# Last layer of a fused four-layer kernel: the 32-point transforms as 32x32 array tiles, and the mode sums placed by VectorE and ScalarE

## The chip, the cores and the metric

The kernel runs on one core of one Trainium2 chip. The metric is the device time in microseconds (us) of one execution. Lower is better.

## The reference, cut to what matters

Four layers in a row, each `x = x + layer(groupnorm(x))` on x of shape (4, 32, 32, 32): a Volterra convolution, a 3x3 convolution, a gated attention layer, and the layer that the change touches, a two-dimensional discrete Hartley transform (DHT) convolution. M is the 32x32 matrix of the transform.

```python
def dht2(x, M1, M2):
    return jnp.einsum('bchw,kh,lw->bckl', x, M1, M2)

def neg_freq(a):
    return jnp.roll(jnp.flip(a, axis=(-2, -1)), shift=(1, 1), axis=(-2, -1))

def compl_mul2d(x1, x2):        # x1: transformed input, x2: weights1 (32, 32, 32, 32)
    x1n, x2n = neg_freq(x1), neg_freq(x2)
    return 0.5 * (einsum('bixy,ioxy->boxy', x1, x2) - einsum('bixy,ioxy->boxy', x1n, x2n)
                  + einsum('bixy,ioxy->boxy', x1, x2n) + einsum('bixy,ioxy->boxy', x1n, x2))
```

The product is transformed back with the same matrix. So for each of the 1024 modes (k, l) a 32-channel input is multiplied by a 32x32 matrix, once for the sum and once for the difference of a mode and its negative.

## The kernel before, in words

The program is written by hand: one instruction list for each engine (TensorE, VectorE, ScalarE, GpSimd, SyncE), tied together by semaphores. Nothing reorders it. Before the last layer come three others; the attention runs from about 90 to 280 us and ends with gates, cell and output of its last pieces. The `keep_clock(bank, n)` helper issues n matmuls of zeros, 128x512 in bf16 (L999), to keep TensorE busy where it would wait.

All of the state is on 128 partitions, image b and one of 32 indices on each group of 32. The last layer alternates a matmul that transforms the index on the partitions with a VectorE transpose of 32x32 blocks that brings the next index there:

- `t1` (L943): two transposes bring h to the partitions. They signal `t1_ready` 1 and 2.
- rows (L1261): for `mt` and `mrt` (the transform and its negative-frequency twin, block diagonal, 128x128), two matmuls of 512 columns each into banks 0 to 3. The i-th matrix signals `rows_done` i+1.
- `t2` (L949): two transposes of 128x1024.
- columns (L1270): for each matrix 16 matmuls with 32 output columns of the array and 256 moving columns, banks 4 to 7. They signal `cols_done` after every eight.
- `tu` (L958): eight transposes of 128x256 give U in `tmp3[:, 3]` and V in `tmp3[:, 4]`.
- mode parts (L458, `mode_part`): V+U and V-U are written into `xm`, a block diagonal tile of 8192 columns that GpSimd zeroed earlier. Each operation covers one 32-partition group g, 32x256 elements. `MODE_STAGES` are the four stages (k2, lh). VectorE makes six operations per stage and GpSimd two (`POOL_MODES = 2`).
- mode matmuls (L1285): in each of the four stages 32 matmuls of 64 columns on two array tiles of 64 columns, as soon as the stage's parts are there (`xm_dve`, `xm_pool`). Stages 0 and 1 end with `mix_done` 1, stages 2 and 3 with `mix_done` 2.
- `y1` (L970): four transposes of 128x1024, two after each `mix_done`. They signal `y1_ready` 1 to 4.
- inverse over l (L1301): five zero matmuls, then 32 matmuls of 256 columns, 16 for each s; each signals `inv_l_done`. The moving operand and the output are both read and written with gaps (last indices of the view: `k` outside `g` outside `s b`).
- `z1` (L976): a transpose of 128x1024 for each s.
- inverse over k (L1309): for each s two matmuls of 512 columns, accumulated; `inv_k_done` for each half.
- last transposes (L982) and the residual sum (L987), in two halves, each half stored by its own DMA.

Every f32 matmul stands in the trace as two records and two weight loads.

Of the kernel before, what the change touches and what calls it, by code (L numbers as in the profile page):

```python
# [45 lines left out]
P = 128  # L46
B, C, H, W = 4, 32, 32, 32
HW = H * W
# [75 lines left out]
POOL_MODES = 2  # L124
# [98 lines left out]
def build(nc, x, consts, wmodes, out):  # L223
    ctx = ExitStack()
    with ctx:  # L225
# [73 lines left out]
        z1 = arena_b[:, 4 * HW:6 * HW]  # L299

# [88 lines left out]
        xm_pool = sem("xm_pool")  # L389
# [58 lines left out]
        def mode_part(engine, k2, lh, g, part):  # L448

            rows = slice(32 * g, 32 * g + 32)

            half = slice(lh * MODES, (lh + 1) * MODES)
            dst = xm[rows].rearrange("p (jh k l) (jl m) -> p jh k (l jl) m", jh=2, k=2, jl=2)[
                :, :, k2, half, 8 * g + 4 * part:8 * g + 4 * part + 4]
            v = tmp3[rows, 4, :].rearrange("p (jh k n b) -> p jh k n b", jh=2, k=2, b=B)[:, :, k2, half]
            u = tmp3[rows, 3, :].rearrange("p (jh k n b) -> p jh k n b", jh=2, k=2, b=B)[:, :, k2, half]
            return engine.tensor_tensor(dst, v, u, ALU.subtract if part else ALU.add)  # L458
# [84 lines left out]
        def _(pool):  # L543
# [68 lines left out]
            pool.wait_ge(tu_ready, 8)  # L612
            pool.wait_ge(xm_zeroed, 1)
            for i, stage in enumerate(MODE_STAGES):
                for g in range(POOL_MODES):
                    if i or g:
                        pool.wait_ge(xm_pool, i * POOL_MODES + g)
                    mode_part(nc.gpsimd, *stage, g, 1).then_inc(xm_pool, 1)

        @block.scalar  # L620
        def _(act):
# [45 lines left out]
            for item in plan:  # L667
# [32 lines left out]
        def _(dve):  # L700
# [246 lines left out]
            for i in range(2):  # L947
                dve.wait_ge(rows_done, i + 1)
                nc.vector.transpose(tmp3[:, 1 + i, :].rearrange("p (c k) -> p c k", k=MODES),  # L949
                                    banks(2 * i).rearrange("p (w c) -> p c w", c=C)).then_inc(t2_ready, 1)  # L950

            for i in range(2):
                src = banks(4 + 2 * i).rearrange("p (b c k jl) -> p b k jl c", b=B, c=C, jl=2)
                dst = tmp3[:, 3 + i, :].rearrange("p (k l jl b) -> p b k jl l", b=B, l=MODES, jl=2)
                for b in range(B):
                    if b % 2 == 0:
                        dve.wait_ge(cols_done, 2 * i + b // 2 + 1)
                    nc.vector.transpose(dst[:, b], src[:, b]).then_inc(tu_ready, 1)  # L958
            dve.wait_ge(tu_ready, 8)
            dve.wait_ge(xm_zeroed, 1)  # L960
            for stage in MODE_STAGES:
                for g in range(4):
                    mode_part(nc.vector, *stage, g, 0).then_inc(xm_dve, 1)
                    if g >= POOL_MODES:
                        mode_part(nc.vector, *stage, g, 1).then_inc(xm_dve, 1)
# [8 lines left out]
            for s in range(2):  # L974
                dve.wait_ge(inv_l_done, s + 1)
                nc.vector.transpose(z1[:, s * HW:(s + 1) * HW].rearrange("p (o h l) -> p o h l", h=2, l=16),  # L976
                                    ps[:, 2 * s:2 * s + 2, :].rearrange("p h (o k) -> p o h k", o=C)
                                    ).then_inc(z1_ready, 1)

            for e in range(2):  # L980
                dve.wait_ge(inv_k_done, e + 1)
                link(nc.vector.transpose(  # L982
                    tmp3[:, 0, :].rearrange("p (k l) -> p l k", l=W)[:, e * W // 2:(e + 1) * W // 2],
                    ps[:, 4 + e, :].rearrange("p (o l) -> p l o", o=C)))
# [6 lines left out]
        def _(pe):  # L991
# [265 lines left out]
            keep_clock(7, 16)  # L1257
            for i, m in enumerate(("mt", "mrt")):
                for e in range(2):
                    pe.wait_ge(t1_ready, e + 1)  # L1260
                    last = mm(ps[:, 2 * i + e, :], c_(m), tmp3[:, 0, e * HALF:(e + 1) * HALF], start=True, stop=True)  # L1261
                last.then_inc(rows_done, 1)

            for i, m in enumerate(("mt", "mrt")):
                pe.wait_ge(t2_ready, i + 1)
                src = tmp3[:, 1 + i, :].rearrange("p (c k) -> p c k", k=MODES)
                for b in range(B):
                    for g in range(4):
                        dst = ps[32 * g:32 * g + 32, 4 + 2 * i + b // 2, (b % 2) * 256:(b % 2 + 1) * 256]
                        last = mm(dst.rearrange("p (c k) -> p c k", k=KG), c_(m)[:, 32 * b:32 * b + 32],  # L1270
                                  src[:, :, KG * g:KG * (g + 1)], start=True, stop=True)
                    if b % 2:
                        last.then_inc(cols_done, 1)

            keep_clock(3, 11)
# [14 lines left out]
            yv = y1.rearrange("p (k jl o g s b) -> p s b jl o g k", k=2, jl=2, o=C, g=4, s=2)  # L1291
            pe.wait_ge(y1_ready, 2)
            keep_clock(0, 5)
            for s, m in enumerate(("mt", "mnt")):
                for jl in range(2):
                    pe.wait_ge(y1_ready, 3 + jl)
                    for jh in range(2):
                        j = 2 * jh + jl
                        zv = ps[:, 2 * s + jh, :].rearrange("p (o g k j) -> p j o g k", g=4, j=2, k=2)
                        for b in range(B):  # L1300
                            last = mm(zv[32 * b:32 * b + 32, jl], c_(m)[:, 32 * j:32 * j + 32], yv[:, s, b, jl],  # L1301
                                      start=(jl == 0), stop=True, skip_group_check=True)
                last.then_inc(inv_l_done, 1)

            for s in range(2):
                pe.wait_ge(z1_ready, s + 1)
                zs = z1[:, s * HW:(s + 1) * HW].rearrange("p (o l) -> p o l", l=W)
                for e in range(2):
                    last = mm(ps[:, 4 + e, :].rearrange("p (o l) -> p o l", o=C), c_(("mt_back", "mnt_back")[s]),  # L1309
                              zs[:, :, e * W // 2:(e + 1) * W // 2], start=(s == 0), stop=(s == 1))  # L1310
                    if s == 1:
                        last.then_inc(inv_k_done, 1)

# [25 lines left out]
def layout_consts(i):  # L1339
# [46 lines left out]
    order = np.arange(MODES).reshape(4, 2, 4).transpose(1, 0, 2).reshape(-1)  # L1386
# [20 lines left out]
```

## Time and profile before

| | |
|---|---|
| median of 3 runs | 336.43 us (334.37 to 336.48) |
| the profiled execution's own time | 334.88 us |
| its span, first to last instruction | 333.1 us |
| mean granted TensorE clock | 0.95 |
| TensorE busy | 294.6 us (88%) |
| VectorE busy | 216.6 us (65%) |
| ScalarE busy | 175.2 us (53%) |
| GpSimd busy | 40.7 us (12%) |

### The profile page before, as it was taken

How to read it: one execution, taken by the hardware profiler on the slowest of the kernel's cores; microseconds unless marked ns; L12 is line 12 of the kernel's file. 1: busy time of each engine (PE TensorE's matmuls, PEld its weight loads, DVE VectorE, ACT ScalarE, POOL GpSimd, SP SyncE). 2: the span in 40 equal slices, each digit the busy share in tenths (PEclk: the TensorE clock that was granted, in tenths of full speed). 3: DMA queues.
4: the chain of work that ended last, by engine and by line, in shares of the span. 5: the costliest groups of instructions: out<-in, count | busy, mean ns of one | idle time of the engine just before them, and what ended most of it. 6: DMA issues, size and time to landing. Idle time of an engine off the chain costs nothing. (4 is left out here: it accounts for less than half of the span.)

```text
span 333.1 us, 9964 instructions
## 1 busy us (share of the span) xinstructions
PE 294.6 (88%) x4276; PEld 136.8 (41%) x4283; DVE 216.6 (65%) x484; ACT 175.2 (53%) x338; POOL 40.7 (12%) x50
## 2 busy tenths in 40 slices
PE   5799979899886499999999999999997998895993
PEld 2477523234313144444444454344342323344831
DVE  3991172478296236687979978888773223779935
ACT  1201101225194279798898989889797983100000
POOL 8400000000000000010101001010200108007000
PEclk9799999999996569999999999999999999997898
DMA  7100000005687559500000000000000000000001
GB/s 230 70 4 4 4 10 0 3 0 162 171 145 113 138 141 293 244 2 5 2 5 2 3 4 2 4 4 2 4 2 4 3 0 2 0 2 2 4 0 63
DMA packets 3471, 15.40 MB, mean 46 GB/s; under 512 B 731, under 2 KB 1547, under 8 KB 2883
## 3 DMA queue, kind: packets, MB, share of 16 engines
q1 hardware_dynamic: 3171, 14.67, 16.3%
q8 instruction: 33, 0.54, 0.7%
q0 software_dynamic: 256, 0.11, 0.2%
q14 instruction: 11, 0.09, 0.1%
HBM read 12.21 MB, written 2.37 MB: 44 GB/s over the span
## 5 line engine op out<-in xcount | busy, mean ns | idle before, releaser
L675 ACT ACTIVATE arena_b<-ps 128x512 f32<-128x512 f32 x232 | 124.9, 609 | 23.7 <-PE ps L1169 22.5
L1140 PE MATMUL ps<-arena_a 72*32 72x450 bf16 x1024 | 91.4, 376 | 4.7 <-DMA arena_a<-q_scratch 4.5
L1169 PE MATMUL ps<-arena_a 75*32 75x512 bf16 x896 | 88.9, 390 | 7.2 <-DMA arena_a<-mt_sb 6.3
L882 DVE TENSOR_REDUCE mx<-ps 128x1 f32<-128x450 f32 x120 | 68.6, 616 | 2.0 <-PE ps L1140 1.9
L877 DVE CUSTOM_DVE_ANT_0 sums<-ps,relus 128x450 bf16<-128x450 f32 x68 | 41.4, 626 | 35.2 <-PE ps L1140 26.8
L1187 PE MATMUL ps<-arena_b,vt 128*32 128x512 f32 x448 | 59.4, 602 | 1.5 <-ACT arena_b L675 1.0
L1140 PEld LDWEIGHTS ps<-arena_a 72*32 72x32 bf16 x1024 | 30.1, 101 | 42.2 <-issue 18.6
L1169 PEld LDWEIGHTS ps<-arena_a 75*32 75x32 bf16 x896 | 25.6, 97 | 52.4 <-ACT arena_b L675 20.6
L683 ACT ACTIVATE relus<-ps 128x450 f32<-128x450 f32 x68 | 37.5, 555 | 9.1 <-PE ps L1140 9.0
L1029 PE MATMUL ps<-arena_a,cst 32*32 32x512 f32 x864 | 30.0, 624 | 2.0 <-ACT arena_a L626 2.0
L999 PE MATMUL ps<-zeros 128*128 128x512 bf16 x82 | 21.3, 397 | 6.5 <-DMA xa<-x 3.5
L1029 PEld LDWEIGHTS ps<-arena_a,cst 32*32 32x32 f32 x864 | 21.4, 105 | 10.2 <-issue 4.9
L1187 PEld LDWEIGHTS ps<-arena_b,vt 128*32 128x32 f32 x448 | 13.8, 111 | 11.9 <-ACT arena_b L675 3.1
L596 POOL DMA_DIRECT2D arena_a<-mt_sb x8 | 5.2, 650 | 105.1 <-DVE mt_sb L891 105.1
L632 ACT ACTIVATE arena_b<-ps 128x512 f32<-128x512 f32 x4 | 2.2, 595 | 28.0 <-PE ps L1029 28.0
L743 DVE SCALAR_TENSOR_TENSOR arena_a<-xp 128x612 f32<-128x612 f32 (+1 forms) x24 | 16.2, 753 | 0.0
L1088 PE MATMUL ps<-arena_b,cst 128*32 128x450 f32 (+1 forms) x144 | 15.9, 565 | 0.0
L999 PEld LDWEIGHTS ps<-zeros 128*128 128x128 bf16 x89 | 8.0, 100 | 18.6 <-issue 7.7
L1285 PE MATMUL ps<-arena_b,arena_a 128*64 128x64 f32 x256 | 10.5, 258 | 4.0 <-DVE arena_a L458 4.0
L603 POOL TENSOR_TENSOR on<-ot,rden 128x512 f32<-128x512 f32 x7 | 7.3, 1039 | 51.6 <-DVE rden L901 51.6
L458 DVE TENSOR_TENSOR arena_a<-arena_a 32x256 f32<-32x256 f32 x24 | 12.9, 563 | 0.5
L899 DVE STREAM_TRANSPOSE ot<-ps 128x512 f32<-128x512 f32 x8 | 5.7, 712 | 10.1 <-PE ps L1193 10.1
(140 smaller groups left out, 237.2 us busy)
## 6 DMA issues: line engine op xcount, KB each, us to landing
arena_b<-wmodes SPq DMA_DIRECT2D x1, 4096.0 KB, 20.5
arena_a<-k_scratch SPq DMA_DIRECT2D x3, 516.8 KB
arena_a<-q_scratch SPq DMA_DIRECT2D x3, 384.0 KB
cst<-consts SPq DMA_DIRECT2D x1, 1045.0 KB, 9.3
k_scratch<-arena_b SPq DMA_DIRECT2D x3, 344.5 KB, 3.7
cst<-consts SPq DMA_DIRECT2D x1, 864.5 KB, 7.2
arena_a<-k_scratch SPq DMA_DIRECT2D x6, 129.2 KB
arena_a<-k_scratch SPq DMA_DIRECT2D x3, 258.4 KB
```

The costliest lines, as they stand in the source:

```text
L458: return engine.tensor_tensor(dst, v, u, ALU.subtract if part else ALU.add)
L675: nc.scalar.activation(probs[:, n % PRING, :], ps[:, SCORE_RING[n % len(SCORE_RING)], :], ACT.Exp).then_inc(expd, 1)
L683: nc.scalar.activation(relus[:, d % 3, :], ps[:, block_bank(i), 0:KHALF], ACT.Relu).then_inc(max_relu, 1)
L743: nc.vector.scalar_tensor_tensor(maps[:, m, n0:n1], xp[:, n0:n1], VOLTERRA_SCALE, xp[:, at + n0:at + n1], ALU.mult, ALU.mult).then_inc(map ...
L877: nc.vector.tensor_tensor_reduce(out=sums[:, d % 2, :], in0=bank, in1=relus[:, d % 3, :], scale=1.0, scalar=-3.0e38, op0=ALU.add, op1=ALU.max,
L882: nc.vector.tensor_reduce(mx[:, a, e:e + 1], bank, AX.X, ALU.max).then_inc(max_read, 1)
L999: mm(ps[:, bank, :], zeros[:, 0:P], zeros[:], start=True, stop=True)
L1029: last = mm(ps[32 * j:32 * j + 32, 2 * b + e, :].rearrange("p (y x) -> p y x", x=W), l0w[r, COL_TILES * i + j, :], window(maps[r, m, :], p ...
L1088: last = mm(ps[32 * b:32 * b + 32, bank + e, 0:ny * cols].rearrange("p (y x) -> p y x", x=cols), weights[:, px, :], window(xst[:, b, :], f ...
L1140: last = mm(ps[32 * j:32 * j + 32, block_bank(i), 0:KHALF], qst[0:PAIR_ROWS, e, g, q0:q0 + 32], kst[0:PAIR_ROWS, g, at:at + KHALF], start= ...
L1169: last = mm(ps[32 * j:32 * j + 32, bank, :], kst[0:S_ROWS, g, k0:k0 + 32], qst[0:S_ROWS, e, g, :], start=True, stop=True)
L1187: last = mm(ps[32 * h:32 * h + 32, bank, :], vt[:, t, half % B * HEADS + h, :], probs[:, (n0 + h) % PRING, :], start=(t == 0), stop=False, ...
```

## The change

Everything before the last layer is left as it was. In the last layer:

- rows: 64 matmuls on 32x32 array tiles, 128 columns each, replace four of 512. Row group b of the array writes bank 4i+b.
- columns: 32 matmuls on 32x32 tiles, 256 columns each, replace 32 that used all 128 rows. `cols_done` comes once for each matrix. The results lie in the upper halves of the eight banks. The zero matmuls behind them now wait for `tu_ready` 4.
- `t2`, `tu`, `z1` and the last transposes read across four banks with other strides. Their number and size are the same.
- mode parts: sum and difference are each made once per stage on 128 partitions (`both_parts`, 128x256 elements, into `xboth`). Then each 32-partition group's 512 elements are copied to their place in `xm` (`placed`): groups 0 and 1 by VectorE, 2 and 3 by ScalarE. GpSimd takes no part.
- inverse over l: 64 matmuls on 32x32 tiles, 128 columns each (`over_l`, 8 in a call). The first two calls need only `y1_ready` 2; ten zero matmuls of 256 columns follow them.
- inverse over k: 32 matmuls on 32x32 tiles, 256 columns each. Both last transposes wait for the same `inv_k_done`.

```diff
-        def mode_part(engine, k2, lh, g, part):
...
-            dst = xm[rows].rearrange("p (jh k l) (jl m) -> p jh k (l jl) m", jh=2, k=2, jl=2)[
-                :, :, k2, half, 8 * g + 4 * part:8 * g + 4 * part + 4]
...
+        def stage_of(tile, k2, lh):
+            return tile.rearrange("p (jh k n m) -> p jh k n m", jh=2, k=2, n=2 * MODES)[
+                :, :, k2, lh * MODES:(lh + 1) * MODES]
+        def both_parts(engine, k2, lh, part):
+            dst = stage_of(xboth, k2, lh)[:, :, :, B * part:B * part + B]
+            return engine.tensor_tensor(dst, stage_of(tmp3[:, 4, :], k2, lh), stage_of(tmp3[:, 3, :], k2, lh),
+                                        ALU.subtract if part else ALU.add)
+        def placed(k2, lh, g):
             rows = slice(32 * g, 32 * g + 32)
+            dst = stage_of(xm[rows].rearrange("p n m -> p (n m)"), k2, lh)[:, :, :, 2 * B * g:2 * B * (g + 1)]
+            return dst, stage_of(xboth[rows], k2, lh)
...
+            act.wait_ge(xm_zeroed, 1)
+            for i, stage in enumerate(MODE_STAGES):
+                act.wait_ge(both_ready, 2 * i + 2)
+                for g in ACT_PLACED:
+                    dst, src = placed(*stage, g)
+                    nc.scalar.activation(dst, src, ACT.Copy).then_inc(xm_act, 1)
...
             for i, m in enumerate(("mt", "mrt")):
                 for e in range(2):
                     pe.wait_ge(t1_ready, e + 1)
-                    last = mm(ps[:, 2 * i + e, :], c_(m), tmp3[:, 0, e * HALF:(e + 1) * HALF], start=True, stop=True)
+                    for q in range(4):
+                        for b in range(B):
+                            r, n = slice(32 * b, 32 * b + 32), slice(16 * 8 * e, 16 * 8 * (e + 1))
+                            last = mm(ps[32 * q:32 * q + 32, 4 * i + b, n].rearrange("p (w c) -> p w c", c=8),
+                                      c_(m)[r, r], t1[r, e * W // 2:(e + 1) * W // 2, 8 * q:8 * q + 8],
+                                      start=True, stop=True)
                 last.then_inc(rows_done, 1)
...
+            pe.wait_ge(tu_ready, 4)
             keep_clock(3, 11)
...
-                pe.wait_ge(xm_dve, (i + 1) * (8 - POOL_MODES))
-                pe.wait_ge(xm_pool, (i + 1) * POOL_MODES)
+                pe.wait_ge(xm_dve, (i + 1) * len(DVE_PLACED))
+                pe.wait_ge(xm_act, (i + 1) * len(ACT_PLACED))
...
+            def over_l(s, k, jl):
+                weights = c_(("mt", "mnt")[s])
+                for jh in range(2):
+                    j = 2 * jh + jl
+                    r = slice(32 * j, 32 * j + 32)
+                    for q in range(4):
+                        dst = ps[32 * q:32 * q + 32, 4 * s + j, 0:256].rearrange("p (b o g k) -> p k (o g) b", b=B, o=8, g=4)
+                        last = mm(dst[:, k], weights[r, r], yv[r, s, k, jl, 8 * q:8 * q + 8].rearrange("p o g b -> p (o g) b"),
+                                  start=True, stop=True)
+                return last
+            over_l(0, 0, 0)
+            over_l(0, 0, 1)
+            for _ in range(10):
+                mm(ps[:, 3, 256:512], zeros[:, 0:P], zeros[:, 0:256], start=True, stop=True)
+            pe.wait_ge(y1_ready, 3)
+            over_l(0, 1, 0)
+            pe.wait_ge(y1_ready, 4)
+            over_l(0, 1, 1).then_inc(inv_l_done, 1)
```

VectorE around the mode parts, before: the last transpose into U and V, the 24 sums and differences, and the transposes behind the mode matmuls.

```order
L958 STREAM_TRANSPOSE arena_a<-ps 128x4x2x32 [waits cols_done]
L958 STREAM_TRANSPOSE arena_a<-ps 128x4x2x32
L458 TENSOR_TENSOR arena_a<-arena_a 32x2x32x4 [waits xm_zeroed,tu_ready]
L458 TENSOR_TENSOR arena_a<-arena_a 32x2x32x4 x23
L970 STREAM_TRANSPOSE arena_b<-ps 128x1024 [waits mix_done]
L970 STREAM_TRANSPOSE arena_b<-ps 128x1024
```

The same place with the change (two of the four stages, then the rows that follow the fourth):

```order
L966 STREAM_TRANSPOSE arena_a<-ps 128x4x2x32 x3
L459 TENSOR_TENSOR arena_b<-arena_a 128x2x32x4 [waits xm_zeroed,tu_ready]
L459 TENSOR_TENSOR arena_b<-arena_a 128x2x32x4
L975 COPY arena_a<-arena_b 32x2x32x8 [waits both_ready]
L975 COPY arena_a<-arena_b 32x2x32x8
L459 TENSOR_TENSOR arena_b<-arena_a 128x2x32x4 x2
L975 COPY arena_a<-arena_b 32x2x32x8 [waits both_ready]
L975 COPY arena_a<-arena_b 32x2x32x8
L980 STREAM_TRANSPOSE arena_b<-ps 128x1024 [waits mix_done]
L980 STREAM_TRANSPOSE arena_b<-ps 128x1024
```

VectorE now has two operations on 128 partitions and two copies on 32 partitions in each stage, where it had six on 32 partitions; a new wait on its own `both_ready` stands ahead of the copies.

TensorE from the last mode stage to the end, before:

```order
L1285 MATMUL ps<-arena_b,arena_a 64x64 [waits xm_pool,xm_dve]
L1285 MATMUL ps<-arena_b,arena_a 64x64 x31
L999 MATMUL ps<-zeros 128x512 [waits y1_ready]
L999 MATMUL ps<-zeros 128x512 x4
L1301 MATMUL ps<-arena_b,cst 32x256 [waits y1_ready]
L1301 MATMUL ps<-arena_b,cst 32x256 x7
L1309 MATMUL ps<-arena_b,cst 128x512 [waits z1_ready]
L1309 MATMUL ps<-arena_b,cst 128x512
```

And with the change:

```order
L1301 MATMUL ps<-arena_b,arena_a 64x64 [waits xm_act,xm_dve]
L1301 MATMUL ps<-arena_b,arena_a 64x64 x31
L1319 MATMUL ps<-arena_b,cst 32x32x4 [waits y1_ready]
L1319 MATMUL ps<-arena_b,cst 32x32x4 x15
L1326 MATMUL ps<-zeros 128x256 x10
L1319 MATMUL ps<-arena_b,cst 32x32x4 [waits y1_ready]
L1319 MATMUL ps<-arena_b,cst 32x32x4 x7
L1319 MATMUL ps<-arena_b,cst 32x32x4 [waits y1_ready]
L1319 MATMUL ps<-arena_b,cst 32x32x4 x39
L1341 MATMUL ps<-arena_b,cst 32x256 [waits z1_ready]
L1341 MATMUL ps<-arena_b,cst 32x256 x15
```

A quarter of the inverse over l has moved ahead of the zero matmuls and no longer waits for the transposes of the second half of the modes. Only eight matmuls stand between `y1_ready` 4 and the first `inv_l_done`.

## Rows read from the trace of the kernel before

**Rows 1.** Chain of waits, last 45 us: start us, us, what.

```profile
299.75 0.41 DVE arena_a L458
...
313.16 2.39 DVE arena_b L970 x2
...
316.85 7.39 PE ps L1301 x62
...
327.06 1.08 DVE arena_a L982
```

**Rows 2.** Timeline, forward transforms: start us, us, engine, instructions [idle before].

```profile
289.74 1.99 DVE L943 STREAM_TRANSPOSE arena_a<-xa 128x512 f32<-128x512 f32 x2
290.84 3.79 PE L1261 MATMUL ps<-arena_a,cst 128*128 128x512 f32 x8 [0.61 <-DVE arena_a L943]
...
292.94 1.25 DVE L949 STREAM_TRANSPOSE arena_a<-ps 128x1024 f32<-128x1024 f32 x1 [1.22 <-PE ps L1261]
...
294.55 3.66 PE L1270 MATMUL ps<-arena_a,cst 128*32 128x256 f32 x64
294.66 1.25 DVE L949 STREAM_TRANSPOSE arena_a<-ps 128x1024 f32<-128x1024 f32 x1 [0.47 <-PE ps L1261]
295.83 3.88 DVE L958 STREAM_TRANSPOSE arena_a<-ps 128x256 f32<-128x256 f32 x8
...
298.37 2.32 PE L999 MATMUL ps<-zeros 128*128 128x512 bf16 x10 [0.16 <-issue]
```

**Rows 3.** Timeline, mode stages.

```profile
299.75 13.38 DVE L458 TENSOR_TENSOR arena_a<-arena_a 32x256 f32<-32x256 f32 x24
299.85 6.94 POOL L458 TENSOR_TENSOR arena_a<-arena_a 32x256 f32<-32x256 f32 x8 [11.45 <-issue]
...
304.58 8.44 PE L1285 MATMUL ps<-arena_b,arena_a 128*64 128x64 f32 x192 [3.89 <-DVE arena_a L458]
...
313.16 4.64 DVE L970 STREAM_TRANSPOSE arena_b<-ps 128x1024 f32<-128x1024 f32 x4
...
313.19 2.09 PE L1285 MATMUL ps<-arena_b,arena_a 128*64 128x64 f32 x64 [0.16 <-DVE arena_a L458]
```

**Rows 4.** Line L458, 299.7:306.3, then 308.2:313.2: ns min/median/max, first and last start.

```profile
L458 DVE TENSOR_TENSOR arena_a<-arena_a x9: 414/834/941, 299.8 to 306.2; 32x256 f32<-32x256 f32 x9
...
L458 DVE TENSOR_TENSOR arena_a<-arena_a x13: 408/415/423, 307.8 to 312.7; 32x256 f32<-32x256 f32 x13
```

**Rows 5.** Stretches, L1285 alone, last L1301: busy (count) PE, PEld, granted clock, DMA, GB/s.

```profile
304.60:308.10 3.50, 3.50 (x64) 3.48 (x64) 0.50 0.00 0
...
313.15:315.30 2.15, 2.09 (x64) 1.95 (x64) 1.00 0.03 8
...
316.80:320.40 3.60, 3.60 (x33) 1.20 (x37) 1.00 0.00 0
```

**Rows 6.** Timeline, inverse transforms.

```profile
316.78 7.46 PE L1301 MATMUL ps<-arena_b,cst 128*32 128x256 f32 x64
...
320.67 1.25 DVE L976 STREAM_TRANSPOSE arena_b<-ps 128x1024 f32<-128x1024 f32 x1 [2.86 <-PE ps L1301]
...
327.06 2.14 DVE L982 STREAM_TRANSPOSE arena_a<-ps 128x512 f32<-128x512 f32 x2 [1.51 <-PE ps L1309]
```

**Rows 7.** Lines by form, matmuls on 32x32 tiles; L1029's starts in 22.64:22.86.

```profile
L1106 PE MATMUL ps<-win,cst 32*32 32x1 f32 x72 | 2.1, 166 | 0.0
...
L1029 PE MATMUL ps<-arena_a,cst x32: 586/587/609, 22.1 to 22.8; 32*32 32x512 f32 x32
...
L1029 PE MATMUL ps<-arena_a,cst 32*32 32x512 f32 x755 | 25.3, 596 | 0.0
```

**Rows 8.** Lines by form, one-source f32 operations, SBUF to SBUF; then PSUM to SBUF.

```profile
L785 DVE TENSOR_SCALAR xb<-xc,cst 128x1024 f32<-128x1024 f32 x1 | 0.7, 742 | 0.0
...
L662 ACT ACTIVATE arena_b<-arena_b 128x512 bf16<-128x512 f32 x2 | 1.3, 630 | 2.4 <-DVE arena_b L822 2.4
...
L748 DVE COPY arena_b<-ps 128x512 f32<-128x512 f32 x4 | 2.6, 686 | 14.1 <-PE ps L1029 14.1
```

More of the change, by code:

```diff
@@ L610, in _ @@
             rsqrt(3)
[L612 to L618, printed above, removed]
         @block.scalar
@@ L948, in _ @@
                 dve.wait_ge(rows_done, i + 1)
-                nc.vector.transpose(tmp3[:, 1 + i, :].rearrange("p (c k) -> p c k", k=MODES),
-                                    banks(2 * i).rearrange("p (w c) -> p c w", c=C)).then_inc(t2_ready, 1)
+                nc.vector.transpose(tmp3[:, 1 + i, :].rearrange("p (b c k) -> p b c k", b=B, k=MODES),
+                                    ps[:, 4 * i:4 * i + 4, 0:256].rearrange("p b (w c) -> p b c w", c=8)
+                                    ).then_inc(t2_ready, 1)
             for i in range(2):
-                src = banks(4 + 2 * i).rearrange("p (b c k jl) -> p b k jl c", b=B, c=C, jl=2)
+                dve.wait_ge(cols_done, i + 1)
                 dst = tmp3[:, 3 + i, :].rearrange("p (k l jl b) -> p b k jl l", b=B, l=MODES, jl=2)
                 for b in range(B):
-                    if b % 2 == 0:
-                        dve.wait_ge(cols_done, 2 * i + b // 2 + 1)
-                    nc.vector.transpose(dst[:, b], src[:, b]).then_inc(tu_ready, 1)
+                    src = ps[:, 4 * i:4 * i + 4, 256 + 64 * b:256 + 64 * (b + 1)].rearrange(
+                        "p q (c k jl) -> p k jl q c", c=8, jl=2)
+                    nc.vector.transpose(dst[:, b], src).then_inc(tu_ready, 1)
             dve.wait_ge(tu_ready, 8)
             dve.wait_ge(xm_zeroed, 1)
[L961 to L965, printed above, removed]
+            for i, stage in enumerate(MODE_STAGES):
+                for part in range(2):
+                    both_parts(nc.vector, *stage, part).then_inc(both_ready, 1)
+                dve.wait_ge(both_ready, 2 * i + 2)
+                for g in DVE_PLACED:
+                    dst, src = placed(*stage, g)
+                    nc.vector.tensor_copy(dst, src).then_inc(xm_dve, 1)
             for k2 in range(2):
@@ L1265, in _ @@
                 pe.wait_ge(t2_ready, i + 1)
-                src = tmp3[:, 1 + i, :].rearrange("p (c k) -> p c k", k=MODES)
-                for b in range(B):
+                src = tmp3[:, 1 + i, :].rearrange("p (n k) -> p n k", k=MODES)
+                for q in range(4):
+                    r = slice(32 * q, 32 * q + 32)
                     for g in range(4):
[L1269 to L1273, printed above, removed]
+                        last = mm(ps[32 * g:32 * g + 32, 4 * i + q, 256:512].rearrange("p (n k) -> p n k", k=KG),
+                                  c_(m)[r, r], src[r, :, KG * g:KG * (g + 1)], start=True, stop=True)
+                last.then_inc(cols_done, 1)
+            pe.wait_ge(tu_ready, 4)
             keep_clock(3, 11)
@@ L1288, in _ @@
                     last.then_inc(mix_done, 1)
-            yv = y1.rearrange("p (k jl o g s b) -> p s b jl o g k", k=2, jl=2, o=C, g=4, s=2)
+            yv = y1.rearrange("p (k jl o g s b) -> p s k jl o g b", k=2, jl=2, o=C, g=4, s=2)
             pe.wait_ge(y1_ready, 2)
[L1293 to L1303, printed above, removed]
+            def over_l(s, k, jl):
[3 more added lines that the diff above has]
+                    r = slice(32 * j, 32 * j + 32)
+                    for q in range(4):
+                        dst = ps[32 * q:32 * q + 32, 4 * s + j, 0:256].rearrange("p (b o g k) -> p k (o g) b", b=B, o=8, g=4)
+                        last = mm(dst[:, k], weights[r, r], yv[r, s, k, jl, 8 * q:8 * q + 8].rearrange("p o g b -> p (o g) b"),
+                                  start=True, stop=True)
+                return last
@@ L1305, in _ @@
+            over_l(0, 0, 0)
[6 more added lines that the diff above has]
+            over_l(0, 1, 1).then_inc(inv_l_done, 1)
+            for k in range(2):
+                over_l(1, k, 0)
+                last = over_l(1, k, 1)
+            last.then_inc(inv_l_done, 1)
             for s in range(2):
@@ L1306, in _ @@
                 pe.wait_ge(z1_ready, s + 1)
[L1307 to L1312, printed above, removed]
+                for q in range(4):
+                    r = slice(32 * q, 32 * q + 32)
+                    for b in range(B):
+                        last = mm(ps[32 * b:32 * b + 32, q, 256:512], c_(("mt_back", "mnt_back")[s])[r, r],
+                                  z1[r, s * HW + 256 * b:s * HW + 256 * (b + 1)], start=(s == 0), stop=(s == 1),
+                                  skip_group_check=True)
@@ L1317, in transform_matrix @@
+                if s == 1:
+                    last.then_inc(inv_k_done, 1)
 def transform_matrix(n):
```

22 lines of the change are left out of this document (11 added, 11 removed).

## The prediction

> **What bounds the kernel now.** I read the chain of waits first, from its end back to 289 us, since all of the change lies in the last layer. The reader is to see that the chain never leaves it: VectorE on L458, the transposes L970, the matmuls L1301, then VectorE again [rows 1]. So one step's end is the next one's start, and each saving counts in full until something else is late. Then I read the timeline for the handovers [rows 2, 3, 6]. Three marks split the layer: A, the start of the mode parts at 299.75; B, `y1_ready` 4 at 313.16 + 4.64 = 317.80; C, the first last transpose at 327.06. What follows C keeps its operations and costs the same.
>
> **Forward transforms.** VectorE is idle 1.22 us ahead of the first L949 and 0.47 ahead of the second [rows 2]. Both gaps are waits for L1261, whose eight records take 3.79 us, or some 0.45 us for 512 columns each; a column costs 0.427/512 us if I take off the record's latency, so 128 columns cost 0.11 and 256 cost 0.21. The change gives the half of the rows that comes last before `rows_done` 1 as 16 matmuls on 16 tiles. Each tile has two passes of 0.11 = 0.21; I add 0.15 for starting 16 of them and 0.16 of latency (a record of a single column takes 166 ns, [rows 7]): 0.52. `t1_ready` 2 comes at 289.74 + 1.99 = 291.73, so `rows_done` 1 comes at about 292.29 instead of 292.94: 0.65 gained. The second matrix is then done by 292.9, long before the first L949 ends at 293.54, so its gap of 0.47 goes. The column matmuls need 0.43 + 0.31 = 0.74 for each matrix and lie beside L949 and L958; one is covered by the second L949 (1.25), the other by four L958 (eight take 3.88). VectorE is the bound from 292.3 on, and A comes at 299.75 - 0.65 - 0.47 = 298.6, **1.1 us** earlier. The coarser `cols_done` costs nothing while L949 covers it. The transposes `t2`, `tu`, `z1` and the last ones now read four banks, for which there is no row; they keep their sizes, so I take their old durations. Their upper end is the 1.0 us that L943 and L982 take for 512 elements (1.99 and 2.14 for two) against 1.25 for 1024 in L949: this is a rival below. Below nothing I see no room, as L949 already moves an element in 1.2 ns.
>
> **Mode stages.** Before, 24 operations take 13.38 us: nine at a median of 834 ns while GpSimd works beside them, then 13 at 415 alone [rows 3, 4]. Now VectorE has per stage two operations of the same length per partition, 2 x 0.41 less a little overlap = 0.76 to 0.82, and two copies of 512 elements. GpSimd is silent, so I take the 415. A copy lies between half of the 742 of L785 (1024 elements), 0.37, and the 0.69 of L748, which reads PSUM; I take 0.45, nearer to L785 because it too goes from SBUF to SBUF. A VectorE stage is 0.80 + 0.03 + 0.90 = 1.7 (2.2 at the upper end). ScalarE starts its two copies when the sums are there, at 0.76, and needs 0.1 for the handover and 2 x 0.6 (L662: 0.63 for 512, [rows 8]), so stage 0 is complete at A + 2.06, and later stages no slower than every 1.7.
>
> That is faster than TensorE. A mode stage takes it 2.09 us at full clock and 3.5 at half [rows 5]. So the **mode matmuls become the bound**: before, they hid behind VectorE. From A: 2.06 + 4 x 2.09 + 0.17 = 10.6 for `mix_done` 2. VectorE finishes its parts at 6.8 and transposes the first half of the modes (2.39, [rows 1]) by 9.2; at the upper end for a copy by 11.2, which would cost 0.6. Then two more L970, 2.4: B = A + 13.0, against 317.80 - 299.75 = 18.05. **5.05 us** gained. TensorE ran its first stage at half clock because it stood idle from 300.7 to 304.58 (3.89 idle, [rows 3]; the zeros end at 298.37 + 2.32, [rows 2]). With the change the 11 zero matmuls start at `tu_ready` 4, about 296.7, and end at 299.0, and stage 0 is ready at 300.7: an idle time of 1.6. I take full clock.
>
> **Inverse transforms.** A pass of 256 columns in L1301 is slow: four concurrent ones take 0.46 (16 such groups in 7.46 us), though L1270 does the same size in 0.23 (3.66 for 16) [rows 2, 6]. L1301 is at clock 1.00 [rows 5], so the gaps in its operands cost a factor of two, and `over_l` still has gaps in its output. The page "SBUF — State Buffer" of the Trainium skill, under "Door 1: The DMA port swizzle", says that any non-contiguous PSUM pattern slows matmuls; the trace agrees, 0.46 to 0.23, and without it the sum would be some 0.2 us smaller. I take 0.21 for a pass of 128 columns here. After `mix_done` 2 TensorE runs two calls of `over_l` (0.6), ten zeros (1.07, half of 10 x 0.21) and one more call by A + 12.5, all before B. Behind B stand one call, 2 x 0.21 + 0.2 = 0.65, then z1 of s=0 (1.25), then z1 of s=1 (1.25; its 32 matmuls take 1.2 beside the first z1), then the accumulation of s=1: two passes of 0.21, 0.15 and 0.16 = 0.74 less what the first half of the passes overlaps, 0.64. With handovers of 0.06, C = B + 3.85, against 327.06 - 317.80 = 9.26: **5.4 us** gained. The last transposes wait for one signal now, not two; before, the second half was ready before the first transpose ended, so nothing changes.
>
> **Sum.** 1.1 + 5.05 + 5.4 = 11.55, so 334.88 - 11.55 = 323.3 for the profiled execution. That one lies 1.55 below the median of the three runs (336.43; they spread from 334.37). I carry half of it: **324.0 us**. My own bounds on this case (copies at 0.69, the gaps, ±0.7 for which of the two levels a run is at) give 322 to 325.8.
>
> **Rival 1, a tile matmul is bound by its start.** On 32x32 tiles L1106 takes 2.1 us for 72 records of one column, 29.6 ns each, though all on one tile in turn; L1029 started 32 records of different tiles in 0.7 us, some 21 ns each, while bound by its 512 columns (755 in 25.3 us, 33.5) [rows 7]. At 29.6 the rows' last half takes 0.95 + 0.17, so `rows_done` 1 gains nothing, and the second matrix needs 1.9, so the gap ahead of the second L949 stays: A loses 1.2 of my 1.1. In the inverse the 32 matmuls of s=1 take 1.9 and are late by 0.6, and the last accumulation takes 1.12, not 0.64. Together 2.3: 325.6 + 0.8 = 326.4 us. The page "TensorE: Matmul & The Clock Gate" of the Trainium skill, under "Back-to-back issue gap", has matmuls never start less than about 25 ns apart, which would bring the time near this case; against it speaks the row of L1029, at 21. Chance 0.26.
>
> **Rival 2, the clock.** Tile matmuls leave TensorE idle more: in the 4 us between 292.9 and 296.7 it would have two bursts of 0.7. If the granted clock falls to half there, as it did after 3.89 us of idleness, the mode stages take 3.5 each: B is 4 x 1.4 = 5.6 later, and 324.0 becomes 329.6. For it: the mode matmuls have lost their cover. Against: the zeros ahead of `t1` and after `tu`. Chance 0.17.
>
> **Rival 3, transposes over four banks cost as L943 and L982 do**, 0.35 us more per 512 elements: t2 1.4, tu 1.4, z1 1.4, so 328.2 us. Chance 0.06.
>
> **Rival 4, slower than before.** Tiles of one array do not run beside each other when each has its own moving operand of 128 columns. Then a record costs its columns, 0.11 or 0.21: rows 10 us behind `t1_ready` 2, columns 13.6, less what L958 hid, so A is 21 later; and 20 more in the inverse: some 363 us. It decides from about 60 ns per record, where 300 records on the path lose the 11.5. L1029 speaks against it: 33.5 ns for 512 columns. Chance 0.03.
>
> **How the numbers follow.** My forecast has 0.48. The range of 8 in 10 runs from 321.5 to 329.8: it leaves out rival 4, the upper end of rival 2 and a little below. A measurement of this kernel can tell about 1% from no change. Every case but the fourth lies more than 1% (3.4 us) below 336.43, so faster 0.94, the same 0.03, slower 0.03.
>
> **What would show it.** Right: the first L956 starts near 292.3 and the second follows without a gap; the two-input operations take 0.41, not 0.83; the mode matmuls stand back to back in four stages of 2.09 at clock 1.0, with VectorE waiting 1 to 2 us ahead of its third L980; from the last L980 to the first L992 some 3.9 us. Wrong: a granted clock of 0.5 between 296 and 312, an L956 that still waits, transposes of over 1.5 us for 1024 elements, a ScalarE copy above 0.7, or something outside the last layer that moves.

## The result and the profile after

The changed kernel takes 322.36 us (median of four runs, 322.16 to 323.37) against 336.44 for the kernel before. The ratio is 0.9602, 95% interval 0.956 to 0.9644. That is 4% faster, and inside the stated range. The profiled execution took 322.51 us with a span of 320.5, against 334.88 and 333.1.

The chain of waits of the changed kernel, last 30 us (start us, us, what), answers to [rows 1]:

```profile
289.23 2.02 DVE arena_a L950 x2
...
291.29 0.67 PE ps L1275 x31
...
291.98 2.38 DVE arena_a L956 x2
294.36 1.06 DVE arena_a L966 x3
...
296.74 3.56 PE ps L1009 x10
...
300.42 7.70 PE ps L1301 x256
...
308.14 2.39 DVE arena_b L980 x2
...
310.58 0.53 PE ps L1319 x23
...
311.13 2.39 DVE arena_b L986 x2
...
313.57 0.88 PE ps L1341 x32
...
314.47 1.05 DVE arena_a L992
```

The long VectorE stretch on the mode parts is gone from it. In its place stand the 256 records of the mode matmuls, and ahead of them the zero matmuls. The timeline of the same kernel answers to [rows 2, 3, 6]; column one is the start in us, column two the length:

```profile
291.98 2.38 DVE L956 STREAM_TRANSPOSE arena_a<-ps 128x1024 f32<-128x1024 f32 x2 [0.74 <-PE ps L1275]
...
296.72 3.58 PE L1009 MATMUL ps<-zeros 128*128 128x512 bf16 x10 [1.43 <-DVE arena_a L966]
...
298.15 0.76 DVE L459 TENSOR_TENSOR arena_b<-arena_a 128x256 f32<-128x256 f32 x2
...
298.94 0.86 DVE L975 COPY arena_a<-arena_b 32x512 f32<-32x512 f32 x2
299.00 1.27 ACT L704 ACTIVATE arena_a<-arena_b 32x512 f32<-32x512 f32 x2 [15.01 <-DVE arena_b L459]
...
300.42 7.68 PE L1301 MATMUL ps<-arena_b,arena_a 128*64 128x64 f32 x256
...
304.91 2.38 DVE L980 STREAM_TRANSPOSE arena_b<-ps 128x1024 f32<-128x1024 f32 x2
...
308.14 2.38 DVE L980 STREAM_TRANSPOSE arena_b<-ps 128x1024 f32<-128x1024 f32 x2 [0.85 <-PE ps L1301]
...
311.13 2.38 DVE L986 STREAM_TRANSPOSE arena_b<-ps 128x1024 f32<-128x1024 f32 x2 [0.61 <-PE ps L1319]
...
314.47 2.11 DVE L992 STREAM_TRANSPOSE arena_a<-ps 128x512 f32<-128x512 f32 x2 [0.96 <-PE ps L1341]
```

The second L956 follows the first without a wait, where there was one of 0.47, and the wait ahead of the first is 0.74 us instead of 1.22. VectorE is done with its copies by 304.9 and with the first two L980 by 307.3, and then waits 0.85 us for TensorE ahead of the third: the bound has changed sides. With the marks of the prediction (t1 start, A first mode part, B end of the fourth y1 transpose, C first last transpose) the two profiled executions compare like this:

| stretch, us | before | after | gain | forecast |
|---|---|---|---|---|
| span start to t1 | 289.74 | 289.23 | 0.51 | 0 |
| t1 to A | 10.02 | 8.92 | 1.10 | 1.1 |
| A to B | 18.05 | 12.38 | 5.67 | 5.05 |
| B to C | 9.25 | 3.95 | 5.30 | 5.4 |

The three stretches give 12.07, and the rest of the 12.6 us of span is the start of the layer. That start is no effect of the change: over the twelve other kernels below, none of which touches anything ahead of the layer, it came anywhere from 288.7 to 295.0 us. So I judge the experiments by their stretches, and the total times only by their intervals. The medians differ by 14.1 us, 2.0 more than the three stretches; nothing here shows that the change earned that rest. Total times of one kernel differ by over 1% between executions on some of the chips used, and the traces of experiments 6 and 12 are of executions 2% above the fastest of their kernel, so that only their stretches are used.

### The profile page after: what moved, and what is told of

Its sections match the earlier page's. It is cut to its first block, busy times and chain, and to the rows that moved or that the text cites. A ratio compares the mean times of both kernels' runs of the same rounds, so it can differ in the third digit from the quotient of the medians.

```text
span 320.5 us, 10448 instructions
## 1 busy us (share of the span) xinstructions
PE 285.3 (89%) x4522; PEld 133.7 (42%) x4528; DVE 209.8 (65%) x476; ACT 180.6 (56%) x346; POOL 34.3 (11%) x42
## 4 chain that ended last, share of the span: by engine, by line
PE 61%; DVE 17%; issue 9%; DMA 6%; ACT 3%; POOL 3%; DVEq 0%; ACTq 0%; POOLq 0%
PE ps L1179 12%; PE ps L1197 11%; PE ps L1150 10%; PE ps L1039 9%; DMA arena_a<-mt_sb 6%; PE ps L1098 4%; ACT arena_b L675 2%; PE ps L1301 2%; PE ps L1086 2%; DVE sums L884 2%; PE ps L1009 2%; PE ps L1254 2%; PE ps L1074 2%; DVE mx L889 1%; PE ps L1203 1%
## 5 line engine op out<-in xcount | busy, mean ns | idle before, releaser
L1179 PE MATMUL ps<-arena_a 75*32 75x512 bf16 x896 | 90.6, 394 | 6.6 <-DMA arena_a<-mt_sb 5.9
L1150 PE MATMUL ps<-arena_a 72*32 72x450 bf16 x1024 | 92.7, 377 | 1.0 <-DVE vrest L854 0.8
L1197 PE MATMUL ps<-arena_b,vt 128*32 128x512 f32 x448 | 60.5, 610 | 1.5 <-ACT arena_b L675 1.0
L1179 PEld LDWEIGHTS ps<-arena_a 75*32 75x32 bf16 x896 | 26.4, 98 | 51.4 <-ACT arena_b L675 21.6
L1039 PE MATMUL ps<-arena_a,cst 32*32 32x512 f32 x864 | 28.6, 596 | 0.8 <-ACT arena_a L626 0.8
L1039 PEld LDWEIGHTS ps<-arena_a,cst 32*32 32x32 f32 x864 | 20.7, 103 | 8.7 <-DMA cst<-consts 1.6
L1098 PE MATMUL ps<-arena_b,cst 128*32 128x450 f32 (+1 forms) x144 | 17.5, 617 | 0.0
L704 ACT ACTIVATE arena_a<-arena_b 32x512 f32<-32x512 f32 x8 | 5.0, 626 | 16.3 <-DVE arena_b L459 16.2
L906 DVE STREAM_TRANSPOSE ot<-ps 128x512 f32<-128x512 f32 x8 | 5.7, 712 | 10.1 <-PE ps L1203 10.1
L755 DVE COPY arena_b<-ps 128x512 f32<-128x512 f32 x4 | 2.6, 686 | 12.6 <-PE ps L1039 12.5
```

Of the source, the lines that this page charges most:

```text
L1039: last = mm(ps[32 * j:32 * j + 32, 2 * b + e, :].rearrange("p (y x) -> p y x", x=W), l0w[r, COL_TILES * i + j, :], window(maps[r, m, :], p ...
L1098: last = mm(ps[32 * b:32 * b + 32, bank + e, 0:ny * cols].rearrange("p (y x) -> p y x", x=cols), weights[:, px, :], window(xst[:, b, :], f ...
L1150: last = mm(ps[32 * j:32 * j + 32, block_bank(i), 0:KHALF], qst[0:PAIR_ROWS, e, g, q0:q0 + 32], kst[0:PAIR_ROWS, g, at:at + KHALF], start= ...
L1179: last = mm(ps[32 * j:32 * j + 32, bank, :], kst[0:S_ROWS, g, k0:k0 + 32], qst[0:S_ROWS, e, g, :], start=True, stop=True)
L1197: last = mm(ps[32 * h:32 * h + 32, bank, :], vt[:, t, half % B * HEADS + h, :], probs[:, (n0 + h) % PRING, :], start=(t == 0), stop=False, ...
```

## The experiments

Each starts from the changed kernel or the kernel before, as said. The ratios are to the kernel before, measured beside it, with the 95% interval.

**1 to 3. Each part of the change undone alone.** The edits put back the old code of that part, shown above in the diff, in the changed kernel.

```diff
 e1_old_parts:   both_parts/placed -> mode_part by VectorE (6 per stage) and GpSimd (2)
 e2_old_forward: 64 + 32 tile matmuls -> 4 (512 columns, 128 rows) + 32 (256 columns, 128 rows), old t2 and tu
 e3_old_inverse: over_l and the tiled inverse over k -> old 32 + 4 matmuls, old z1, last transposes, constants
```

> The changed kernel with the old making of the mode parts: 24 operations on 32 partitions by VectorE and 8 by GpSimd. Theory (VectorE's 13.4 us were the bound, the mode matmuls are now): the stretch from the first mode part to y1_ready 4 goes from 12.4 back to about 18.0 us, so some 5.7 us more than the changed kernel, near 328.2 us, ratio to the kernel before 0.977. Rival (most of the gain came because the zero matmuls now start later and keep the clock up until the mode matmuls): the stretch grows by less than 2 us, near 324 us, ratio 0.965.

> The changed kernel with the old rows and columns (four matmuls of 512 columns, 32 with all 128 rows) and their transposes. Theory (the tiles gain 1.1 us ahead of the mode parts, since two VectorE waits of 0.65 and 0.47 go): 1.1 us more, near 323.9 us, ratio 0.963; from the first t1 transpose to the first mode part 10.0 us instead of 8.9. Rival (the tiles gain nothing here, as VectorE is the bound of the forward part, and they let the clock fall to half ahead of the mode stages): the same or a shorter time than the changed kernel, ratio 0.958 to 0.960.

> The changed kernel with the old inverse: 32 matmuls of 256 columns with all rows for l, four of 512 for k, old transposes and old order of the constants. Theory: from y1_ready 4 to the first last transpose 9.2 us again instead of 3.95, so 5.3 us more than the changed kernel, near 328.0 us, ratio 0.976. Rival (part of the inverse's gain belongs to starting a quarter of it early, and the clock is low in it): less than 3.5 us more, ratio below 0.970.

| | t1 to A | A to B | B to C | ratio to before |
|---|---|---|---|---|
| changed kernel | 8.92 | 12.38 | 3.95 | 0.960 [0.956, 0.964] |
| old parts | 8.90 | 18.06 | 3.95 | 0.976 [0.967, 0.984] |
| old forward | 10.01 | 12.38 | 3.95 | 0.971 [0.963, 0.979] |
| old inverse | 9.06 | 12.38 | 9.16 | 0.985 [0.977, 0.993] |

Each part changes its own stretch, by 5.68, 1.09 and 5.21 us, and the others by at most 0.15. So in the stretches the three gains add up (11.98 of 12.07), and each is shown as an effect of its own part. The rivals fall: the mode stage's gain is not the clock's, as it vanishes with the old parts although the zeros still start late, at 297.86 here. VectorE's 24 operations then run without a break, and TensorE waits for them (timeline of the kernel with the old parts):

```profile
297.86 4.10 PE L1001 MATMUL ps<-zeros 128*128 128x512 bf16 x11 [0.89 <-DVE arena_a L960]
299.68 13.39 DVE L459 TENSOR_TENSOR arena_a<-arena_a 32x256 f32<-32x256 f32 x24
...
304.52 5.76 PE L1293 MATMUL ps<-arena_b,arena_a 128*64 128x64 f32 x128 [2.56 <-DVE arena_a L459]
```

The totals of the second and third lie above what was expected (0.963 and 0.976). In the third the whole layer starts at 293.5 in the profile, 4.3 us later than in the changed kernel, in work that the edit doesn't touch. In the second the profiled execution took 323.38 us, near the 323.9 expected, and the others up to 327.35; where these lost their time no trace shows.

**4. VectorE places all four groups, ScalarE none.**

```diff
-DVE_PLACED = (0, 1)
-ACT_PLACED = (2, 3)
+DVE_PLACED = (0, 1, 2, 3)
+ACT_PLACED = ()
```

> The changed kernel with all four groups placed by VectorE and none by ScalarE. Theory (the mode matmuls are the bound by a small margin: 1.92 us a stage against 1.69 for VectorE): a VectorE stage becomes 0.79 + 4 x 0.43 = 2.5 us, VectorE is the bound again, the last stage is complete 10.1 us after the first part instead of 7.1, and the first half of the modes is transposed by 12.4 instead of being finished early: y1_ready 4 comes 2.4 us later, near 325.3 us, ratio 0.967. Rival (the matmuls or the handovers set the pace whatever VectorE does): within 0.5 us of the changed kernel, ratio 0.960 to 0.962.

A to B is 15.01, 2.63 more than with ScalarE's help (2.4 expected). The ratio is 0.979 [0.973, 0.986], above the 0.967 expected; the layer starts at 293.6 in this profile, 4.4 us later than in the changed kernel. Four copies take 1.77 us and a stage 2.59, above TensorE's 1.92, and the four y1 transposes then follow each other without a wait. VectorE is the bound again. B to C is 0.32 longer; the granted clock fell to 0.50 near 320.7 in that execution, while the last accumulation ran, which may be why.

**5 and 6. No zero matmuls ahead of the mode stages**, in the changed kernel and in the kernel before.

```diff
             pe.wait_ge(tu_ready, 4)
-            keep_clock(3, 11)
```

> The changed kernel without the eleven zero matmuls ahead of the mode stages. TensorE then stands idle from 295.3 to 300.3, 5 us. Theory (the mode matmuls are the bound, and their clock counts): the granted clock is 0.5 in the first mode stages, a stage takes about 3.5 us instead of 1.92 while it lasts, and the time grows by 1.6 us for each stage at half clock: 3 to 6 us, near 327.5 us, ratio 0.974. Rival (the mode matmuls have slack behind VectorE and ScalarE): less than 0.7 us more.

> The kernel before without the eleven zero matmuls ahead of the mode stages. Its VectorE needs 3.4 to 4.1 us a stage, so mode matmuls at half clock (3.5 us a stage) hide. Theory: under 0.6 us of difference, ratio 0.998 to 1.002, although more mode stages run at half clock. Rival (the clock was on the path in the kernel before too): 1.5 us or more.

In the changed kernel TensorE stands idle for 4.66 us, and the mode matmuls start at half clock (stretches of their line: PE and PEld busy, granted clock, DMA, GB/s):

```profile
303.80:306.80 3.00, 3.00 (x56) 3.00 (x58) 0.50 0.02 5
306.90:311.40 4.50, 4.50 (x161) 4.50 (x159) 1.00 0.01 4
```

A to B grows from 12.38 to 13.75, by 1.37. The half clock held for the first 3.07 us of the mode matmuls: 56 records came in 3.00 us, where the changed kernel needs 1.68 for 56 (256 in 7.68). The expected 3 to 6 us supposed two to four stages at half clock, and it was less than one. The four executions took 323.3, 323.3, 327.1 and 327.1 us; ratio 0.967 [0.961, 0.974]. The traced one is of the longer pair, and its layer starts 3.4 us later than in the changed kernel. In the kernel before, A to B stayed at 18.06 without the zeros, and the ratio is 0.999 [0.995, 1.003]. The 128 records of mode matmuls below are its first two stages, and the clock was 0.50 from 306.9 to 313.7, so 3.9 us of them were at half clock, against 5.5 us in the kernel before (304.58 to 310.1). So the edit did not bring the longer half clock that was expected, but the two amounts differ by 1.6 us, and A to B was the same to 0.01 us. Mode matmuls had slack before and have none now (timeline of the kernel before without zeros, then the stretch of L1285 in the kernel before that follows the one in [rows 5]):

```profile
305.00 13.38 DVE L458 TENSOR_TENSOR arena_a<-arena_a 32x256 f32<-32x256 f32 x24
318.41 4.64 DVE L970 STREAM_TRANSPOSE arena_b<-ps 128x1024 f32<-128x1024 f32 x4
...
309.83 5.84 PE L1284 MATMUL ps<-arena_b,arena_a 128*64 128x64 f32 x128 [6.36 <-DVE arena_a L458]
```

```profile
308.20:310.10 1.90, 1.90 (x36) 1.85 (x36) 0.50 0.03 9
```

**7. Zeros earlier, so that the clock does not fall.** In the changed kernel the granted clock was 0.50 from 295.84 to 299.25, and the zeros took 3.58 us.

```diff
                         last = mm(... columns ...)
+                for _ in range((2, 8)[i]):
+                    last = mm(ps[:, 4 * i, 0:256], zeros[:, 0:P], zeros[:, 0:256], start=True, stop=True)
                 last.then_inc(cols_done, 1)
...
-            keep_clock(3, 11)
+            keep_clock(3, 15)
```

> The changed kernel with two zero matmuls of 256 columns behind the columns of the first matrix, eight behind those of the second (ahead of its signal), and fifteen instead of eleven of 512 after that. Theory: TensorE has no gap over 0.6 us from the rows to the mode stages, the granted clock stays 1.0, the zeros end at about 299.7, and the mode stages start at the same 2.1 us after the first mode part, since the parts are what they wait for: 0.0 to 0.2 us gained over the changed kernel. Rival (the half clock of 296 to 299 costs the changed kernel 1 us or more): a gain of 1 us or more. Third: with the clock already low the longer zeros run to 302 and cost up to 2 us.

The clock stayed at 1.0 until 317.0. The mode matmuls start 2.28 us after A, as in the changed kernel (2.27), and A to B is 12.38 again. t1 to A is 9.25, 0.34 more, since the eight zeros ahead of the signal hold up the transposes behind it. Ratio 0.961 [0.957, 0.965]. So the half clock in the forward part cost the changed kernel nothing that more zeros could bring back, and this edit loses what it spends. The kernel with the old forward part says the same: its clock stayed at 1.0 until 315.9, and its A to B is 12.38 too.

**8 and 9. The rows in matmuls of 64 columns**, twice as many; first with the two halves one after the other on the same tile, then with the halves as the outer loop.

```diff
-  mm(ps[32q.., 4 * i + b, 128 e ...], c_(m)[r, r], t1[r, 16 e:16 (e + 1), 8q..])
+  for w in range(16 * e, 16 * (e + 1), 8):      # e9: inside q, b; e12: outside q, b
+      mm(ps[32q.., 4 * i + b, 8 * w:8 * w + 64], c_(m)[r, r], t1[r, w:w + 8, 8q..])
```

> The changed kernel with the rows in twice as many matmuls of 64 columns (128 of them, 256 records). A look at what bounds a group of 16 tile matmuls. Theory A (starts: 13 to 14 ns a record whatever the columns): the records of one matrix's half take twice the time, the last 96 records of 128 columns (1.32 us apart from the latency) become 192 in 2.6 us, and the second t2 transpose waits about 0.7 us. Theory B (columns: two passes of 0.11 us for each tile): the stretch stays at 1.3 to 1.5 us.

> As the kernel with the rows in twice as many matmuls of 64 columns, but two matmuls in a row never lie on the same array tile (the two halves of the columns are the outer loop). Theory A (a record costs its start, 12.7 to 13.8 ns, whatever its columns and its neighbour): the last 192 records of the rows start within 2.4 to 2.65 us, the second t2 transpose waits about 0.6 to 0.8 us. Theory B (two in a row on one tile were what made the earlier kernel slow, and the columns count): 1.2 to 1.5 us for the 192, no wait. The earlier kernel's stop of TensorE of 1.3 us in mid-stream, with nothing that the profile shows to wait for: if it belongs to the larger number of instructions, it comes again here; if to chance, not.

In both, TensorE stopped in mid-stream after the same record, the 177th (timeline of the second, then of the first):

```profile
289.81 2.29 PE L1276 MATMUL ps<-arena_a,cst 32*32 32x64 f32 x177 [0.62 <-DVE arena_a L950]
...
293.77 0.96 PE L1276 MATMUL ps<-arena_a,cst 32*32 32x64 f32 x75 [1.67 <-issue]
```

```profile
292.72 2.67 PE L1276 MATMUL ps<-arena_a,cst 32*32 32x64 f32 x177 [0.61 <-DVE arena_a L950]
296.66 1.13 PE L1276 MATMUL ps<-arena_a,cst 32*32 32x64 f32 x74 [1.27 <-issue]
```

From t1 to A these kernels need 11.41 us (halves one after the other) and 12.05 (spread), against 8.92; each was run once, with 327.48 and 325.48 us.

Between the first records and the stop the starts are 13.5 ns apart in the first kernel (112 starts in 1.51 us) and 10.1 in the second (112 in 1.13), against 12.7 for 128 columns in the changed kernel (96 in 1.22). So half the columns do not take half the time: in the spread order twice the records cost 1.6 times. The order counts too, as 13.5 against 10.1 shows. Neither theory holds as written, and no single price for a start fits either. In the changed kernel the first 32 records take 0.51 us with some 0.27 for the last one, so they start 8 ns apart, with the same 128 columns and the same order as the 96 behind them:

```profile
290.33 0.51 PE L1275 MATMUL ps<-arena_a,cst 32*32 32x128 f32 x32 [0.62 <-DVE arena_a L950]
291.29 1.49 PE L1275 MATMUL ps<-arena_a,cst 32*32 32x128 f32 x96 [0.45 <-DVE arena_a L950]
```

What slows the longer streams was not tested. The stop, 1.3 us idle in the first kernel and 1.7 in the second, comes again at the same record, so it belongs to the program, by its length or place, and not to chance. The profile names nothing that TensorE waited for. A load of instructions (16 KB, 1.0 and 1.4 us) begins some 1 us before it, at 294.3 in the first and 291.15 in the second, but whether it is the cause was not tested.

**10 and 11. Which side of the old inverse over l was slow.** In the kernel before, the reading or the writing of L1301 is made dense. The layer's output is then not the reference's. Each was run once (334.77 and 337.04 us), so only the stretches count.

```diff
 e7_read_dense
-   ... yv[:, s, b, jl], start=(jl == 0) ...
+   ... y1[:, 256 * b:256 * b + 256], start=(jl == 0) ...
 e8_write_dense
-   zv = ps[:, 2 * s + jh, :].rearrange("p (o g k j) -> p j o g k", g=4, j=2, k=2)
+   zv = ps[:, 2 * s + jh, :].rearrange("p (j o g k) -> p j o g k", g=4, j=2, k=2)
```

> The kernel before, but each matmul of the inverse over l reads 256 neighbouring columns of y1 instead of its gapped view; so that layer's output is not the reference's. The output view keeps its gaps of two. Theory A (the gapped reading makes a pass cost 0.46 us instead of 0.23): the 64 records take 3.7 to 3.9 us instead of 7.46. Theory B (the gapped PSUM output does): 7.4 us as before.

> The kernel before, but each matmul of the inverse over l writes 256 neighbouring columns of its bank, in another order than the transposes behind it expect; so that layer's output is not the reference's. The reading keeps its gaps. Theory A (reading): 7.4 us as before. Theory B (writing): 3.7 to 3.9 us.

Groups by line, dense reading first, dense writing second (busy us, mean ns of one):

```profile
L1301 PE MATMUL ps<-arena_b,cst 128*32 128x256 f32 x64 | 3.9, 382 | 0.0
```

```profile
L1301 PE MATMUL ps<-arena_b,cst 128*32 128x256 f32 x64 | 7.5, 633 | 0.0
```

The gapped reading from SBUF costs the factor of two, and the gap of two in the PSUM output nothing (B to C is 9.25 with the dense writing). The edit removes all gaps of the reading at once, so which of them costs is open. B to C falls from 9.25 to 5.66 with the dense reading, so that alone is worth 3.6 us, against the 5.3 of the whole new inverse. Beside that kernel the changed one is 0.58 us faster from B to the first z1 transpose, 0.60 over the two z1 transposes and 0.54 from there to C. How much of the first belongs to the quarter of the inverse that starts early was not tested.

**12. The kernel before without GpSimd in the mode parts** (`POOL_MODES = 0`).

> The kernel before with all 32 mode parts made by VectorE and none by GpSimd. Theory (VectorE loses as much to GpSimd at its side, 0.83 us instead of 0.41 for an operation, as GpSimd takes off it): 32 x 0.39 = 12.6 us instead of 13.4, the first stage is there at 3.2 us instead of 4.8: 0.8 us faster, ratio 0.998. Rival (GpSimd was a help, and the gain of the change is only in the fewer operations): 24 operations cost 9.5 us and eight more 3.2, so slower or the same, ratio 1.000 or above.

A to B is 17.18, 0.87 less than before; ratio 0.997 [0.992, 1.002]. All 32 operations by VectorE take 12.50 us, 24 of them beside GpSimd took 13.38:

```profile
304.97 12.50 DVE L458 TENSOR_TENSOR arena_a<-arena_a 32x256 f32<-32x256 f32 x32
```

GpSimd's help was worse than none, but its removal is only 0.87 of the 5.67. With experiment 4 the rest can be read too: from 17.18 to 15.01 (2.17) for making sums and differences on 128 partitions with VectorE placing them all, and from there to 12.38 (2.63) for giving half of the placing to ScalarE.

## Why the prediction was right

**The bound and the marks.** All of the gain lies on the chain that was named, in the three stretches that were named, and the three undoings add up.

**Forward.** 1.1 forecast, 1.10 measured, and 1.09 when undone. That they agree so closely is in part luck. The first L956 starts 2.75 us after t1 starts (2.55 forecast, 3.21 before), so the term for the rows brought 0.46 and not 0.65: the 0.52 from `t1_ready` 2 to `rows_done` 1 had too little latency in it. The second L956 follows at once, as forecast, and the pair and the L966 are 0.17 us shorter than their old durations, which fills the hole. `t2` and `tu` over four banks cost no more: 1.19 per L956 of a pair, 3.83 for eight L966 (3.88 before).

**Mode stages.** The mechanism held: VectorE no longer sets the pace, and it waits for TensorE. The size was off by 0.6 us to the good side. The term "4 x 2.09" took the length of one stage with its last record's latency in it; back to back the four take 7.68, 1.92 each, which explains 0.68. The 0.17 added behind them was the latency once more, where 0.02 passed until the third L980. Against it, stage 0 started at A + 2.27, not 2.06: ScalarE's two copies took 1.27, and TensorE began 0.15 after them. A VectorE copy took 0.416 (0.45 taken), the first two-input operations 0.42, as without GpSimd.

**Inverse.** 5.4 forecast, 5.30 measured. One step of its reasoning failed without hurting the sum: "the gaps in its operands cost a factor of two, and `over_l` still has gaps in its output". Experiments 10 and 11 show that the output's gaps cost nothing in the old inverse; the old reading did it. The sentence of the Trainium skill's page "SBUF — State Buffer" under "Door 1: The DMA port swizzle", which I had said the trace bears out, is not borne out for an output with a step of two; there the measurement decides. The output of `over_l` has a larger gap (its last index has a step of 64 words), and no run made that one dense. But two calls of it, 32 records, took 0.50 us, as the first 32 of the rows with their dense output did (0.51). So I see no cost of the gap there either, and the 0.21 for a pass of 128 columns was too much. That the call behind B took 0.61 to the first z1 transpose, near the 0.65 taken, is then luck: the 0.2 beside the passes was too little. The last accumulation took 0.88 and not 0.64, as nothing of it overlapped; the two z1 transposes took 2.38 and not 2.50, which gives back a part.

**Rival 1** (starts 29.6 ns apart) did not happen: 12.7 ns at 128 columns, 10.1 at 64, and 8 in the first 32 records. L1106's row, all on one tile in turn, was the wrong neighbour. The figure of about 25 ns from the page "TensorE: Matmul & The Clock Gate" of the Trainium skill, under "Back-to-back issue gap", is not a floor for records on different 32x32 tiles here. The row that I set against it was misread: 32 starts from 22.1 to 22.8 lie some 23 ns apart, not 21, and with starts given to 0.1 us it could not tell 21 from 25.

**Rival 2** (the clock) did happen in part, which the forecast did not say, and it was one of my own signs of being wrong: the granted clock was 0.50 from 295.84 to 299.25. It fell before the zeros, after TensorE had run only two bursts of column matmuls (0.73 and 0.88 us) since 292.8, and of all TensorE's work only zeros ran in it. They took 3.58 us instead of 2.35 and ended at 300.30, when stage 0's parts had just come, at 300.27. So it cost 0.1 us at most. "I take full clock" held for the mode stages (1.00 from 300.4 to 308.1) with 1.2 us to spare, and that margin is luck rather than forecast. In the kernel of the spread rows the half clock lasted to 303.19. Its last zeros ran on to 303.3, 0.4 us past the parts of stage 0 (ready at 302.89), and A to B was 12.66 (timeline of that kernel from 300 us on, TensorE alone):

```profile
299.79 3.57 PE L1009 MATMUL ps<-zeros 128*128 128x512 bf16 x8
303.30 7.68 PE L1301 MATMUL ps<-arena_b,arena_a 128*64 128x64 f32 x256
```

Where it reaches into the mode stages, experiment 5 gives the price: 1.37 us for 3.07 us at half clock. The 5.6 us that I gave this rival supposed half clock for all four stages; no run showed that.

**Rival 3** is out by the transposes above. **Rival 4** fell with the first row of tiles.

**The total.** 323.3 for the profiled execution against 322.51 measured: 0.6 from the mode stages, 0.5 from the layer's start and the rest the other way. The half of 1.55 that I carried to the median (it gives 324.1, where I wrote 324.0) went the wrong way, as the median of the changed kernel lies below its profiled execution. So the median came out 1.6 us below the forecast, and only 0.5 of that is in the layer's three stretches.

## What to carry to other kernels

When a chain hands over between two engines at every step, look for the step that becomes late next; here the mode matmuls went from slack to bound, and half clock on them went from free to 0.45 us per us. Work that is cut into pieces of 32 partitions can be done once on 128, with only the placing left for the pieces and split over two engines; here that brought 2.17 and 2.63 us. Before rewriting slow matmuls, make first the reading and then the writing dense in a throwaway version: here it was the reading alone, and it made 3.6 us of the old time. When parts of a sum come from neighbouring rows, look at each part afterwards: two of the three sums here came out right through errors that cancelled.

## What the runs showed of the hardware that I had not expected

- In streams of some 100, f32 records on different 32x32 tiles start 10.1 ns apart at 64 columns and 12.7 at 128, with 13.5 when two matmuls in a row share a tile (64 columns). The first 32 records of 128 columns start 8 ns apart.
- A TensorE stream of 256 such records stopped for 1.3 and 1.7 us after its 177th record, in two kernels, with nothing to wait for in the profile; the changed kernel's stream of 128 did not. The cause is open.
- A gapped view as the moving operand (last index with a step of 2048 words, 8 in the index before it) takes f32 matmuls on four column tiles to nearly twice the time of a dense one (633 against 382 ns a record, 7.5 against 3.9 us for all); a step of two words in the output costs nothing.
